# Loading and splitting the conditioning blocks earlier, and splitting more gate weights ahead, at the end of the conditioning stage

## The reference

```python
c    = x @ W.T + b + 2.0 * (x @ A[slot]) @ B[slot]      # conditioning; one lora slot per sequence, rank 16
gate = silu(c @ W_gate.T)                              # D_FF = 1376
up   = c @ W_up.T
x    = x + (gate * up) @ W_down.T
```

## Time and profile before

| | |
|---|---|
| median of 3 runs | 1027.36 us (1024.82 to 1027.88) |
| the profiled execution | 1025.09 us, its span 1023.3 us |
| TensorE matmuls | 1000.8 us busy, 98% of the span |
| TensorE weight loads | 835.3 us, 82% (beside the matmuls) |
| VectorE | 565.5 us, 55% |
| ScalarE | 412.3 us, 40% |
| GpSimd | 189.7 us, 19% |
| TensorE clock granted, mean | 0.997 of full speed |
| DMA | 210.17 MB, mean 205 GB/s |

### The profile page before, as it was taken

How to read it: one execution, slowest core, us unless ns; L and a number is a source line. 1 busy time by engine, 2 the same in 40 slices (tenths; PEclk the granted TensorE clock), 3 DMA queues, 4 the chain that set the end, 5 groups by cost and what they waited for, 6 DMA issues and landing times.

```text
span 1023.3 us, 13768 instructions
## 1 busy us (share of the span) xinstructions
PE 1000.8 (98%) x4795; PEld 835.3 (82%) x4795; DVE 565.5 (55%) x979; ACT 412.3 (40%) x780; POOL 189.7 (19%) x172
## 2 busy tenths in 40 slices
PE   9999967999999999999999999999999999999998
PEld 7888866888888888888888888888878688888887
DVE  5554545878685332487323397232394357666663
ACT  4645446565571333472333373333354132322210
POOL 5132301555400112310112230111350000000000
PEclk9999989999999999999999999999999999999999
DMA  9797735776877767767866777876796402222211
GB/s 329 291 326 279 258 123 213 279 261 228 298 246 248 232 190 195 249 231 256 260 195 194 231 232 258 276 190 194 193 339 230 151 1 83 93 83 83 93 42 62
DMA packets 111403, 210.17 MB, mean 205 GB/s; under 512 B 12260, under 2 KB 12260, under 8 KB 111080
## 3 DMA queue, kind: packets, MB, share of 16 engines
q1 hardware_dynamic: 108800, 200.88, 60.1%
q0 software_dynamic: 2400, 8.41, 2.2%
q10 hardware_dynamic: 136, 0.01, 0.0%
HBM read 154.20 MB, written 55.05 MB: 204 GB/s over the span
## 4 chain that ended last, share of the span: by engine, by line
PE 84%; DVE 9%; DMA 3%; ACT 1%; issue 1%; SPq 1%; POOL 0%; DVEq 0%; ACTq 0%; POOLq 0%
PE bank L1389 83%; DVE op_lo L1110 3%; DVE cop_lo L1096 2%; DMA c<-c_scratch 1%; DMA wring<-wd_scratch 1%; PE bank L1552 1%; PE bank L1413 1%; DVE h_lo L1115 0%; DMA wu_raw<-in_w_up 0%; ACT cop_hi L807 0%; DMA w_raw<-in_w 0%; DVE c L1101 0%; DVE c L1094 0%; DVE s L1143 0%; DVE c_t L1092 0%
## 5 line engine op out<-in xcount | busy, mean ns | idle before, releaser
L1389 PE MATMUL bank<-cop_hi,wring 128*128 128x512 f32 x1234 | 381.3, 389 | 5.2 <-ACT bank L832 2.8
L1389 PEld LDWEIGHTS bank<-cop_hi,wring 128*128 128x128 f32 x1234 | 231.6, 188 | 54.8 <-ACT bank L832 3.7
L1389 PE MATMUL bank<-cop_lo,wring 128*128 128x512 f32 x616 | 239.7, 389 | 0.0
L1389 PE MATMUL bank<-op_hi,wring 128*128 128x512 f32 x560 | 174.0, 389 | 0.8 <-DMA wring<-wd_scratch 0.8
L1124 DVE TENSOR_TENSOR v<-bank,p7s 128x512 f32<-128x512 f32 x44 | 30.4, 692 | 197.1 <-PE bank L1389 197.1
L1389 PEld LDWEIGHTS bank<-cop_lo,wring 128*128 128x128 f32 x616 | 115.6, 188 | 23.9
L1389 PEld LDWEIGHTS bank<-op_hi,wring 128*128 128x128 f32 x560 | 105.1, 188 | 23.3 <-DMA wring<-wd_scratch 1.2
L1389 PE MATMUL bank<-op_lo,wring 128*128 128x512 f32 x280 | 108.9, 389 | 0.0
L657 POOL TENSOR_TENSOR h_t<-h,h 128x512 f32<-128x512 f32 x20 | 26.3, 1316 | 383.9 <-DVE h L1143 383.9
L1110 DVE TENSOR_TENSOR op_lo<-h,op_hi 128x512 fp32r<-128x512 f32 x100 | 73.5, 754 | 6.8 <-ACT op_hi L822 6.8
L863 ACT ACTIVATE s<-bank 128x512 f32<-128x512 f32 x44 | 26.3, 598 | 122.2 <-PE bank L1389 122.2
(11 more groups left out here) (177 smaller groups left out, 1695.6 us busy)
## 6 DMA issues: line engine op xcount, KB each, us to landing
wring<-wgu_scratch SPq DMA_DIRECT2D x231, 256.0 KB, 2.9
wring<-wd_scratch SPq DMA_DIRECT2D x140, 256.0 KB, 4.7
wgu_scratch<-wring SPq DMA_DIRECT2D x77, 256.0 KB, 2.6
x_raw<-in_x SPq DMA_DIRECT2D x32, 256.0 KB, 6.7
c_scratch<-c_out SPq DMA_DIRECT2D x32, 256.0 KB, 2.4
c<-c_scratch SPq DMA_DIRECT2D x32, 256.0 KB, 4.1
raw<-x_scratch SPq DMA_DIRECT2D x32, 256.0 KB, 3.8
out<-res SPq DMA_DIRECT2D x32, 256.0 KB, 2.0
```

Of the source, the lines that this page charges most:

```text
L1389: return e.matmul(out_ap, lhs, rhs, start=start, stop=stop, skip_group_check=True)
```

## The change

Five things change, all at the seam between stages 1 and 2:

- `load_c(0, 0)` is issued after the stores of tile 5, ahead of the first gate weights; `load_c(0, 1)` at the start of tile 7's stores.
- In tiles 6 and 7, all seven `cop_split` of a half stand behind `lora_in(t)` and ahead of the closings `close_c(t, m)` on ScalarE, and so do the `cop_rest` on VectorE.
- `LEAD` is 12: the whole chunk 0 (seven weights) is split at the end of tile 6, five weights of chunk 1 at the end of tile 7.
- SP stores the seven weights of chunk 0 ahead of tile 7's blocks of c and then loads chunk 2; it no longer waits there until all of c is stored.
- Two waits are added: `begin_y` of the first chunk waits for the last closing, and `product_1` of the first chunk waits until all of c is stored (its destination h11 lies over c_out).

```diff
-    LEAD = 10
+    LEAD = 12
@@
-    def cop_due(t, m):
-
-        part = {(NT - 2, 1): (0, 4), (NT - 2, 2): (4, 7), (NT - 1, 1): (7, 11), (NT - 1, 2): (11, 14)}.get((t, m), (0, 0))
-        return cop_order[part[0]:part[1]]
+    def cop_due(t):
+
+        return cop_order[7 * (t - NT + 2):7 * (t - NT + 3)] if t >= NT - 2 else []
+
+    def g_due(t):
+
+        return {NT - 2: range(0, 7), NT - 1: range(7, LEAD)}.get(t, range(0))
@@ SP
+            if t == NT - 1:
+                for n in g_due(NT - 2):
+                    store_gate_up(n)
+                load_gate_up(2)
+                load_c(0, 1)
             for m in range(KC):
                 e.wait_ge(c_closed, nth(t, m))
...
-                if t == NT - 2 and m in (0, 3):
-                    load_c(0, m // 3)
-
-        for m in range(KC):
-            e.wait_ge(c_stored[m], DMA * NT)
-        for n in range(N_G):
+            if t == NT - 3:
+                load_c(0, 0)
+
+        for n in range(7, N_G):
             store_gate_up(n)
@@ ScalarE, begin_y
+            if n == 0:
+                e.wait_ge(c_closed, nth(NT - 1))
@@ ScalarE, tile t (VectorE likewise, with cop_rest and gate_up_lo)
+            for q, i in cop_due(t):
+                cop_split(0, q, i)
             for m in range(KC):
                 close_c(t, m)
                 for n in d_due(t, m):
                     down_hi(n)
-                for q, i in cop_due(t, m):
-                    cop_split(0, q, i)
-                if m == 3 and t >= NT - 2:
-                    for n in range(5 * (t - NT + 2), 5 * (t - NT + 3)):
-                        gate_up_hi(n)
+            for n in g_due(t):
+                gate_up_hi(n)
@@ VectorE, product_1
+            if n == 0:
+                for m in range(KC):
+                    e.wait_ge(c_stored[m], DMA * NT)
```

More of the change, by code:

```diff
@@ L1293, in dve_program @@
             lora_in(t)
+            for q, i in cop_due(t):
+                cop_rest(0, q, i)
             for m in range(KC):
@@ L1296, in dve_program @@
                     down_lo(n)
[L1297 to L1301, removed]
+            for n in g_due(t):
+                gate_up_lo(n)
         e.wait_ge(small_in, 3 * DMA)
```

## The result

The changed kernel takes 1021.33 us (median of 7 runs), the kernel before 1027.36: a ratio of 0.9941, with a 95% interval of 0.9923 to 0.9958, some 6 us less. One of the seven runs took 1108.99 us at a granted clock of 0.851 and is left out of the ratio; the other six lie between 1020.11 and 1022.47. The profiled execution took 1020.27 us, with a span of 1018.5, 4.8 less than before. I had forecast 1016.1, in a range of 1012.5 to 1020.5. The direction is right, the time is above the range, and half of the gain isn't there.

A forecast was written before the change was run, and what follows sets the result against it. TensorE was taken as the bound, busy 98% of the span, with 13.2 us idle in 118 to 182 us. Gains of 9.25 + 2.04 = 11.3 us gave 1013.8 profiled, 1016.1 as median, range 1012.5 to 1020.5.

The forecast's parts named there:

- Parts 1 and 2: End of tile 6: c lands by about 124.5; VectorE's chain behind lora_in(6) ends its low parts at 136.7.
- The collision: VectorE's c chain beside GpSimd's gate sums: each sum costs VectorE 0.45 us, five ahead of the last sum 2.25.
- The new wait at cond_base(7, 0): Start of tile 7: close_c(6, 0), queued behind operand 4's split, makes TensorE stand about 1.7 us.
- The hole ahead of lora_in(7): Conditioning, tile 7: this hole and the slow clock go, 9.7 us, with 0.3 us to spare.
- Part 3: Tile 7 and first gates: c lands at 146.7, product 6 starts at 156.75 instead of 165.99, gaining 9.25 us.
- The hole ahead of the first gate product: Ahead of product 1: TensorE stands 1.15 us until c of tile 7 is closed.
- The hole ahead of product 6: Behind products 1 and 7: TensorE stands 1.35 us until begin_y is done.
- Part 4: Chunk 1, at 178.44: the 2.04 us hole ahead of product 6 goes, as chunk 2's load goes out near 140.
- Part 5: Gate products of set 0: LEAD 12 equals the ring's 12 slots; copies delayed 0.31 to 0.41 us cost nothing, 0.3 spare.
- regular short holes in chunks 2 to 9: Gate products of set 0: a named sign, in TensorE's timeline, that the forecast is wrong.
- My rival for "slower": Chunks 0 to 8: with LEAD 12 the high part ahead of begin_z awaits a late raw block; chance 0.05.
- The new queue is dearer: Conditioning's end: 0.74 us a sum, first hole 3.2, c of tile 7 late; 1018.4 to 1021.4 us, chance 0.18.

The follow-up runs named there:

- Experiment 4: The changed kernel with load_c(0, 1) issued ahead of the seven stores instead of behind them; 1017.82 us, ratio 0.99.
- experiment 3: The changed kernel with GpSimd's h sums held until sum_c22 of the even chunk, in all sets; 1022.95 us, ratio 0.9945.
- experiment 5: The changed kernel with load_c(0, 1) ahead of the seven stores and h sums held until sum_c22 in set 0 only, chunks 2 to 8; 1013.65 us.
- Experiment 1: The changed kernel with LEAD back at 10, the rest of the change kept; 1017.9 us, ratio 0.9893.
- experiment 6: The changed kernel with LEAD 10 and load_c(0, 1) ahead of the seven stores, h sums not held; 1012.15 us, ratio 0.9837.
- experiment 2: The kernel before with LEAD 12 alone (five weights behind tile 6, seven behind tile 7); 1036.26 us, ratio 1.0083.

## Why the prediction was wrong, step by step

**Parts 1 and 2 were right, to 0.3 us.** All of this execution runs 0.8 us late from about 20 us on (lh_lo(6) at 125.94 for 125.14), where nothing was changed; times below have to be read with that. The first c blocks were issued at 118.57, where the gate weights had been, and didn't hold VectorE up (c_t at 126.55, behind lh_lo). The collision was as priced: the five sums ahead of the last c sum cost 2.22 us for 2.25. The last c sum was over 6.43 us after c_t started (132.98), for a forecast of 6.46; the chain took 10.97 (to 137.52), for 10.8:

```profile
126.55 0.68 DVE L1099 TENSOR_TENSOR c_t<-c,c 128x512 f32<-128x512 f32 x1
127.27 1.12 DVE L1101 TENSOR_TENSOR c<-c,c 128x512 f32<-128x512 f32 x1
128.32 1.23 DVE L1103 TENSOR_TENSOR cop_lo<-c,cop_hi 128x512 fp32r<-128x512 f32 x1
...
137.52 0.41 DVE L1086 TENSOR_TENSOR wring<-wg_raw,wring 128x256 fp32r<-128x256 f32 x1
```

The new wait at cond_base(7, 0) is there: 1.43 us idle for "about 1.7", by a closing queued behind a split. The hole ahead of lora_in(7) went from 7.96 to 0.3 (the forecast had 0.3 to spare), and the slow clock behind it with it.

**Part 3: one term too small.** The hole ahead of the first gate product was 2.56, for 1.15. The term was the landing of c of tile 7. I had SP's last issue at 142 and c by 146.7; the stores left the queue 0.54 apart, the last c issue was at 144.62 and c_t could start at 149.18 (148.4 without the late start: 1.7 late). Experiment 4 shows that it is the order of SP's queue. The hole ahead of product 6 (1.35) didn't come, because the slow clock gave begin_y its time: products 1 and 7 took 4.2 us for 2.7. In experiment 3, with the same late start (154.79) and the clock full, they are over at 157.82, a hole of 1.02 ended by begin_y follows, and product 6 starts at 158.84, for 158.87 here. So the slow clock cost nothing of its own. Up to product 6 the gain is 7.1 us (158.87 for 165.99), for 9.25; 0.8 of what is missing is the late start.

**Part 4 was right.** Product 6 of chunk 1 follows without a hole, at 168.9 (the second of the two matmuls that the timeline joins from 168.67 on). Before it was 178.44: 9.5 us gained so far, for a forecast of 11.3. With that gain the median would have been 1017.9, inside the range.

**Part 5 is the step that failed:** "Cost nothing, with 0.3 to spare". Four holes cost some 5 us of the 9.5; at the first matmul behind the gate products of set 0 (266.45 for 271.10) 4.7 is left, and 4.8 in the spans. The prediction had named regular short holes in chunks 2 to 9 as a sign of being wrong, and these are they. I had checked the copies that product 6 and product 5 wait for, and they do hold: no hole is there. I hadn't followed ScalarE's later high parts to silu2, and from there VectorE's queue to sum_c22, which has five low parts in it. GpSimd's h sums beside these low parts stood at nothing in the sum, with no reason given: part 2 prices GpSimd's weight sums, and nowhere the h sums of set 0. My rival for "slower" looked at the same parameter in the wrong place, late raw blocks; in fact the blocks come earlier against sum_c22, and that frees GpSimd to collide. The collision is shown: without it (experiments 3 and 5) the holes go with LEAD 12. That LEAD matters is shown as well (four, one and no holes), but not by which way: the 0.85 us by which silu2 comes late, or the GpSimd sums that meet the low parts. Experiment 1 says that LEAD 10 alone isn't enough, with load_c behind the stores. Its chunks 2 and 6 differ from 4 and 8, and from experiment 6, by 0.1 to 0.8 us in when the weight sums start against silu2. GpSimd starts them when a raw block lands; why the blocks land so, and why load_c first moves them, stays open.

**The number fits a rival whose mechanism didn't come.** 1021.33 lies in what "The new queue is dearer" gives, 1018.4 to 1021.4. But its price of 0.74 a sum and its first hole of 3.2 us are not there (0.44 and 1.43); only c of tile 7 came as late as it says. That its time fits is chance.

## What to carry to other kernels

When a ring is filled up to its last slot, the producer no longer runs ahead: each of its instructions waits for what the consumer did last. Follow everything queued behind the producer's instructions, on its engine and on the next one, and not only the first copy. A transfer or a product made earlier also frees the engines behind it earlier; ask what these then run beside. And when an experiment's time shows nothing, look in its trace whether the loss went or moved.

## What the runs showed of the hardware

**VectorE beside GpSimd.** A subtraction of 128x256 takes 0.41 us alone, 0.96 beside GpSimd sums of 128x256 (0.74 alone) and 1.51 beside sums of 128x512 (1.29 alone, 1.35 to 1.47 there). Of 128x512 it takes 0.69 alone and up to 1.24 beside 128x256. What is added, 0.55 and 1.10, is GpSimd's instruction less about 0.2. So a VectorE instruction that is small pays as much as a large one, and several small ones ahead of a critical sum are a poor neighbour of h sums. A sum with one operand from a PSUM bank (L1136 at 175.99 in the changed kernel) stays at 0.68 beside a GpSimd sum that starts at 175.87. The Trainium skill (SBUF — State Buffer, section "Who interferes with whom") has the loser wait for the whole instruction, and an instruction with one SBUF input not wait at all: these rows agree with the second, and nearly with the first.

**The clock behind a short hole varies.** The same hole ahead of the first gate product was 2.56 us in the changed kernel, 2.62 in experiment 1 and 2.50 in experiment 3, with the same instructions around it. The granted clock of 154.5 to 158.5 was 0.61, 0.70 and 1.00:

```profile
154.50:158.50 4.00, 3.82 (x11) 3.07 (x12) 3.70 (x11) 4.00 (x11) 0.00 (x0) 0.61 0.78 288
```

```profile
154.50:158.50 4.00, 3.94 (x12) 3.17 (x13) 3.66 (x10) 3.78 (x10) 0.00 (x0) 0.70 0.80 299
```

```profile
154.50:158.50 4.00, 3.03 (x12) 2.17 (x12) 3.70 (x10) 4.00 (x11) 0.00 (x0) 1.00 0.74 276
```

These are the busy times by stretch of the changed kernel, experiment 1 and experiment 3. A hole of some 2.5 us may or may not cost the clock; one of 2.04 (the kernel before) and those of 1.4 didn't in any run here, and one of 5.30 (0.59 behind it, experiment 2) and of 8.0 (0.57, the kernel before) did.
